# An attention tower on one core: ones beside x in the weighing products, the projection one step later, and the second variance on ScalarE

## What is computed

```
h = tok(x)                      # 16 -> 512 (silu) -> 256, plus a linear residual 16 -> 256
h = h + attention(layernorm(h)) # 16 heads of 16 over the 64 tokens of a sequence, then W_out
h = h + ffn(layernorm(h))       # fft -> complex matrix -> ifft: one real 256 x 256 product, plus bias
```

## Time and profile before

| | |
|---|---|
| median of 3 runs | 142.65 us (142.65 to 142.79) |
| the profiled execution | 142.76 us |
| its span, first to last instruction | 141.0 us |
| mean granted TensorE clock | 0.993 |
| busy: PE, PEld | 132.8 us, 112.4 us |
| busy: DVE, ACT, POOL | 111.6, 85.7, 94.7 us |

### The profile page before, as it was taken

The page is one execution under the profiler, slowest core; times in us unless marked ns, Lnnn a source line. Parts: engine busy times, 40 slices in busy tenths (PEclk is TensorE's granted clock), DMA queues, the critical chain, the costliest instruction groups (busy, mean ns, idle before and its releaser), DMA issues.

```text
span 141.0 us, 6132 instructions
## 1 busy us (share of the span) xinstructions
PE 132.8 (94%) x2444; PEld 112.4 (80%) x2444; DVE 111.6 (79%) x337; ACT 85.7 (61%) x245; POOL 94.7 (67%) x186
## 2 busy tenths in 40 slices
PE   6879999999999998999999999999999999999861
PEld 2469999999997876978878889889788788788540
DVE  5584596859978578798898898988988988978751
ACT  4374765477878584865947747649558477455110
POOL 3284796996583364677687686786876876773361
PEclk9999999999999999999999999999999999999997
DMA  4678000030000010121312302203113123031102
GB/s 70 157 174 257 14 0 0 0 36 11 2 0 5 5 19 5 19 50 15 63 37 23 60 12 49 56 7 65 46 15 60 37 23 59 6 60 41 38 0 74
DMA packets 24508, 5.89 MB, mean 42 GB/s; under 512 B 20384, under 2 KB 24224, under 8 KB 24480
## 3 DMA queue, kind: packets, MB, share of 16 engines
q1 hardware_dynamic: 24192, 5.37, 18.3%
q10 hardware_dynamic: 288, 0.13, 0.3%
HBM read 2.35 MB, written 2.10 MB: 32 GB/s over the span
## 4 chain that ended last, share of the span: by engine, by line
PE 78%; DVE 7%; POOL 4%; issue 3%; DMA 3%; ACT 1%; SPq 1%; POOLq 0%; DVEq 0%
PE bank L1036 11%; PE bank L954 11%; PE bank L1022 7%; PE bank L1099 6%; PE bank L1075 5%; PE bank L959 5%; PE bank L1080 4%; PE bank L1120 4%; PE bank L1064 3%; DMA wf_raw<-in_W_r 3%; PE bank L1049 2%; PE bank L1133 2%; PE bank L948 2%; PE bank L1103 2%; PE bank L1124 2%
## 5 line engine op out<-in xcount | busy, mean ns | idle before, releaser
L824 DVE TENSOR_REDUCE bank<-bank 128x4 f32<-128x256 f32 x64 | 22.8, 425 | 6.9 <-ACT pT L376 6.5
L376 ACT ACTIVATE pT<-bank 128x256 f32<-128x256 f32 x64 | 19.4, 391 | 2.5 <-PE bank L1049 2.5
L1036 PE MATMUL bank<-qT,xzT 32*128 32x64 f32 x512 | 17.9, 276 | 0.0
L1036 PEld LDWEIGHTS bank<-qT,xzT 32*128 32x128 f32 x512 | 15.7, 186 | 2.7 <-issue 2.7
L695 DVE TENSOR_TENSOR hid_lo<-bank,hid_hi 128x512 fp32r<-128x512 f32 x16 | 11.0, 685 | 7.5 <-ACT bank L344 7.5
L582 POOL TENSOR_TENSOR side_lo<-sideT,side_hi 128x256 fp32r<-128x256 f32 x14 | 10.2, 728 | 8.3 <-ACT sideT L386 8.3
L545 POOL TENSOR_SCALAR xblk<-xh,parity_sb 128x128 f32<-128x128 f32 x32 | 11.5, 372 | 5.9 <-PE bank L1080 4.8
L371 ACT ACTIVATE maxT<-bank 128x128 fp32r<-128x128 f32 x16 | 4.4, 277 | 17.8 <-PE bank L1058 17.8
L593 POOL TENSOR_TENSOR on_lo<-onT,on_hi 128x256 fp32r<-128x256 f32 x14 | 10.3, 737 | 7.1 <-ACT on_hi L390 6.8
L553 POOL TENSOR_TENSOR hb_all<-h_all,bout_bc 128x256 f32<-128x256 f32 x16 | 11.5, 735 | 4.0 <-ACT h_all L348 4.0
L361 ACT ACTIVATE xzT<-bank,parity_sb 128x256 f32<-128x256 f32 x28 | 12.0, 498 | 0.0
(11 more groups left out here) (166 smaller groups left out, 386.8 us busy)
## 6 DMA issues: line engine op xcount, KB each, us to landing
out<-y SPq DMA_DIRECT2D x16, 128.0 KB, 1.7
xblk<-xh SPq DMA_DIRECT2D x32, 32.0 KB, 2.5
wo_raw<-in_W_o SPq DMA_DIRECT2D x1, 512.0 KB, 4.2
wout_raw<-in_W_out SPq DMA_DIRECT2D x1, 256.0 KB, 2.9
fr<-in_wr SPq DMA_DIRECT2D x1, 256.0 KB, 4.3
fi<-in_wi SPq DMA_DIRECT2D x1, 256.0 KB, 4.3
minus_raw<-in_minus_rows SPq DMA_DIRECT2D x1, 128.0 KB, 2.2
bout_bc<-in_b_out SPq DMA_DIRECT2D x1, 128.0 KB, 3.5
```

The costliest lines, as they stand in the source:

```text
L376: nc.scalar.activation(pT[:, j, :], bank[j][:, D:2 * D], ACT.Exp).then_inc(exp_done, 1)
L824: nc.vector.tensor_reduce(rowmax[:, j, :], bank[j][:, 0:D].rearrange("p (h k) -> p h k", k=TOK), AX_X, ALU.max).then_inc(max_done, 1)
L1036: pe.matmul(bank[j][:, at0:at0 + TOK], xzT[t % 3][rows32, 2 * half + b, :, :].rearrange("p e k -> p (e k)"), qT[t % 3][rows32, half, TOK * ...
```

## The change

The change does the following.

- In `weigh` the separate row sums go. `xblk` keeps ones in the 16 columns beside each head's 16 columns of x, so each product gives the weighted x and the row sum together. The products are now 64 rows deep, one for each head e of a pair: 32 with 64 columns in place of 16 with 64 and 4 with 256. They write two banks. All of `xblk` is placed by four DMAs a tile; `place_same` on GpSimd goes.
- The division: VectorE transposes all 512 columns at once and takes reciprocals (`invert`), GpSimd multiplies (`divide`; VectorE from tile 14 on), VectorE transposes back (`turn_on`). The two small steps on VectorE, spread and multiply, go.
- `project(i)` moves from the middle of step i to the start of step i+1, directly behind `weigh(i+1)`. `mix_freq` and `finish` move back a step or more: mix_freq(i-2), finish(i-3). `turn_max` stands between `scores` and `keyed_scores`, and `turn_side` ahead of `weigh`. Tiles 14 and 15 are caught up in step 15 and behind it.
- The variance of h2 goes from VectorE (`variance2`) to ScalarE, in two passes with an accumulated sum: `sum_row`, then `sum_squares` with the negative mean as a per-partition bias; `mean2` on GpSimd stands between them.
- The order in a step changes on ScalarE and GpSimd too, and `xh`, `h2b`, `rstd2` get a third buffer.

```diff
...
-        X_BANK, PV_BANK, MAX_BANK, PROJ_BANK = 4, 5, 6, 7
-        FREQ_BANK, SIDE_BANK, QUERY_BANK = PROJ_BANK, MAX_BANK, X_BANK
-        rowmax = bank[MAX_BANK][:, P:P + 4 * QUADS].rearrange("p (j h) -> p j h", h=4)
+        PV_BANK = (5, 6)
+        QUERY_BANK, SIDE_BANK, MAX_BANK, PROJ_BANK, FREQ_BANK = 4, 4, PV_BANK[1], 7, 7
+        rowmax = score_banks[:, :, 0:4]
...
+        def turned_x(t):
+            return bank[4][:, 0:D] if t < 3 else bank[PV_BANK[0]][:, D:2 * D]
...
-            def place_crossed(t):
+            def place(t):
                 sp.wait_ge(xh_set, t + 1)
                 if t >= 2:
                     sp.wait_ge(pv_done, t - 1)
+                heads = xh[t % 3][:].rearrange("p (g e d) -> p g e d", e=2, d=HD)
                 for b in range(2):
...
+                    for e in range(2):
+                        sp.dma_start(xblk[t % 2][TOK * e:TOK * e + TOK, b, :, 0:HD],
+                                     heads[TOK * b:TOK * b + TOK, :, e, :]).then_inc(xblk_placed[t % 2], 16)
+            sp.wait_ge(blocks_set, 2)
+            place(0)
+            place(1)
+            for i in range(T + 3):
                 if i + 2 < T:
-                    place_crossed(i + 2)
-                if i >= 1:
-                    store(i - 1)
+                    place(i + 2)
+                if i >= 3:
+                    store(i - 3)
...
+            def sum_row(t):
+                act.wait_ge(h2_done, t + 1)
+                if t >= 1:
+                    act.wait_ge(mean2_done, t)
+                    act.wait_ge(squares2_done, t)
+                nc.scalar.activation(unread[:], h2[t % 2][:], ACT.Copy, accum_out=sum2[:]).then_inc(sum2_done, 1)
+            def sum_squares(t):
+                act.wait_ge(mean2_done, t + 1)
+                act.wait_ge(sum2_done, t + 1)
+                if t >= 1:
+                    act.wait_ge(ve2_done, t)
+                nc.scalar.activation(unread[:], h2[t % 2][:], ACT.Square, bias=neg_mean2[:],
+                                     accum_out=squares2[:]).then_inc(squares2_done, 1)
             def step(i):
+                if i + 3 < T:
+                    copy_xT(i + 3)
                 if i + 1 < T:
                     copy_max(i + 1)
+                if i + 3 < T:
+                    copy_xzT(i + 3)
+                if i >= 1:
+                    sum_row(i - 1)
+                if i + 1 < T:
+                    exponent(i + 1)
+                if i < WHOLE_ON:
+                    lead_on(i)
+                if i + 3 < T:
+                    copy_q(i + 3)
                 if i >= 1:
                     copy_side(i - 1)
-                if i + 3 < T:
-                    copy_xT(i + 3)
-                    copy_xzT(i + 3)
-                if i < WHOLE_ON:
-                    lead_on(i)
-                if i + 1 < T:
-                    exponent(i + 1)
-                if i + 3 < T:
-                    copy_q(i + 3)
+                    sum_squares(i - 1)
...
-            def place_same(t):
...
+            def mean2(t):
+                pool.wait_ge(sum2_done, t + 1)
+                if t >= 1:
+                    pool.wait_ge(squares2_done, t)
+                nc.gpsimd.tensor_scalar(neg_mean2[:], sum2[:], -1.0 / D, None, ALU.mult).then_inc(mean2_done, 1)
             def inv_std2(t):
-                pool.wait_ge(mv2_done, t + 1)
-                nc.gpsimd.tensor_scalar(ve2[:], mv2[:, 1:2], EPS, None, ALU.add).then_inc(ve2_done, 1)
-                if t >= 2:
-                    pool.wait_ge(y_set, t - 1)
+                pool.wait_ge(squares2_done, t + 1)
+                if t >= 1:
+                    pool.wait_ge(rstd2_done, t)
+                nc.gpsimd.tensor_scalar(ve2[:], squares2[:], 1.0 / D, EPS, ALU.mult, ALU.add).then_inc(ve2_done, 1)
+                if t >= 3:
+                    pool.wait_ge(y_set, t - 2)
...
+            def divide(t):
+                pool.wait_ge(inv_done, t + 1)
+                nc.gpsimd.tensor_tensor(on_rows[:].rearrange("p c e d -> p e c d"), weighedT[:, :, :, 0:HD],
+                                        inv_sum[:].unsqueeze(3).to_broadcast([P, 2, D // 32, HD]),
+                                        ALU.mult).then_inc(on_divided, 1)
             def step(i):
-                if i + 2 < T:
-                    place_same(i + 2)
                 if i == 0:
                     split_mix_weights()
-                if 1 <= i <= WHOLE_SIDE:
-                    split_side(i - 1)
+                if i < WHOLE_ON:
+                    divide(i)
+                if 2 <= i <= WHOLE_SIDE + 1:
+                    split_side(i - 2)
+                if 2 <= i <= T:
+                    inv_std2(i - 2)
+                if 1 <= i < T:
+                    add_bias(i - 1)
+                    mean2(i - 1)
+                if i + 4 < T:
+                    normalize(i + 4)
                 if i < WHOLE_ON:
                     split_on(i)
                 if i == T:
+                    mean2(i - 1)
                     add_bias(i - 1)
                     inv_std2(i - 1)
-                elif i >= 1:
-                    inv_std2(i - 1)
-                    add_bias(i - 1)
-                if i + 4 < T:
-                    normalize(i + 4)
...
+            def invert(t):
+                dve.wait_ge(pv_done, t + 1)
+                if t >= 1:
+                    dve.wait_ge(on_divided, t)
+                nc.vector.transpose(weighedT[:].rearrange("p e c r -> p e (c r)"), weighed[:, :, 0:D]).then_inc(pv_turned, 1)
+                dve.wait_ge(pv_turned, t + 1)
+                nc.vector.reciprocal(inv_sum[:], weighedT[:, :, :, HD]).then_inc(inv_done, 1)
             def divide(t):
-                dve.wait_ge(pv_done, t + 1)
-                nc.vector.transpose(sumsT[:], bank[PV_BANK][:, D:2 * D]).then_inc(sums_turned, 1)
...
                 dve.wait_ge(inv_done, t + 1)
...
+                if t == WHOLE_ON:
+                    dve.wait_ge(on_set, t)
+                nc.vector.tensor_tensor(on_rows[:].rearrange("p c e d -> p e c d"), weighedT[:, :, :, 0:HD],
+                                        inv_sum[:].unsqueeze(3).to_broadcast([P, 2, D // 32, HD]),
+                                        ALU.mult).then_inc(on_divided, 1)
+            def turn_on(t):
+                dve.wait_ge(on_divided, t + 1)
                 if t >= 1 and t - 1 < WHOLE_ON:
                     dve.wait_ge(on_lo_set, t)
                 elif t >= 1:
                     dve.wait_ge(proj_done, t)
-                nc.vector.tensor_tensor(onT[:].rearrange("p a t -> p (a t)"), bank[PV_BANK][:, 0:D],
-                                        inv_rows[:], ALU.mult).then_inc(on_set, 1)
+                nc.vector.transpose(onT[:].rearrange("p a t -> p (a t)"),
+                                    on_rows[:].rearrange("p c e d -> p (c e d)")).then_inc(on_set, 1)
...
-            def variance2(t):
...
             def step(i):
-                if i < T:
+                invert(i)
+                if i >= WHOLE_ON:
                     divide(i)
                 if i >= 1:
-                    variance2(i - 1)
+                    residual(i - 1)
+                if i >= 3:
+                    finish(i - 3)
+                turn_on(i)
                 if i + 3 < T:
                     split_x(i + 3)
                 if i + 2 < T:
                     for j in range(QUADS):
                         maximum(i + 2, j)
                     split_max(i + 2)
-                if i < T:
-                    residual(i)
-                if i >= 1:
-                    finish(i - 1)
-
...
+            finish(T - 3)
+            residual(T - 1)
+            finish(T - 2)
+            finish(T - 1)
...
             def weigh(t):
                 pe.wait_ge(exp_done, QUADS * (t + 1))
-                pe.wait_ge(xblk_same, t + 1)
-                pe.wait_ge(xblk_crossed[t % 2], 32 * (t // 2 + 1))
+                pe.wait_ge(xblk_placed[t % 2], 64 * (t // 2 + 1))
                 if t == 0:
                     pe.wait_ge(h_copied, T)
-                for j in range(QUADS):
-                    pe.matmul(bank[PV_BANK][32 * j:32 * j + 32, D:2 * D], pair_ones[:], pT[:, j, :], start=True, stop=True)
                 for half in range(HALF):
                     for b in range(2):
                         cols = slice(half * P + TOK * b, half * P + TOK * (b + 1))
-                        for j in range(QUADS):
-                            last = pe.matmul(bank[PV_BANK][32 * j:32 * j + 32, cols],
-                                             xblk[t % 2][:, b, half * P + 32 * j:half * P + 32 * j + 32],
-                                             pT[:, j, cols], start=True, stop=True)
+                        for e in range(2):
+                            for j in range(QUADS):
+                                last = pe.matmul(bank[PV_BANK[e]][32 * j:32 * j + 32, cols],
```

(62 more changed lines are left out.)

128 lines of the change are left out of this document (49 added, 79 removed).

## The result

The changed kernel takes 146.94 us (median of 4 runs, 146.17 to 148.26), the kernel before 142.65 on the same chip: ratio 1.0303, 95% interval 1.0239 to 1.0366. It is slower. The forecast was slower too, at 144.5, but the time lies just outside its range of 140.8 to 146.9. The profiled execution took 146.17 with a span of 144.4; outside the span lie 1.77 us, as before. Executions over 1.5% above the fastest of the same kernel are left out of ratios and medians.

What follows compares the result with a forecast made beforehand. TensorE bounds the kernel, in flight 94% of the span, 5.56 us a step. Span 141.0 + 0.1 (steps) - 1.2 (filling) + 3.0 (emptying) = 142.9, with 1.76 around it 144.66, so about 144.5; range 140.8 to 146.9.

Steps and rivals of the forecast that it cites:

- Filling: Start of the pipeline, to the weighing of tile 13: 1.2 us earlier than before, bounds 0 and 2.
- Emptying: From the end of weighing 13 to the last y: 19.45 us against 16.45, +3.0, bounds +1.5 and +3.8.
- Placing: Four placing DMAs a tile in SyncE's queue, 2.5 us: covered by up to 5.27 - 2.5 us of room, costing nothing.
- The loop that I expect to set the step: Two-step loop through ScalarE, VectorE and GpSimd to project: 11.13 us, 5.57 a step, so TensorE waits at on_lo.
- TensorE in the change: TensorE's own pieces in a step: 5.56 - 0.44 + 0.15 = 5.27 us, up to 5.74.
- 64 x 7 ns = 0.43: Weighing's 64 new instructions on eight array pieces, at half of 14 ns each: 0.43 us, other bound 0.90.
- 0.15 for the change of pieces: TensorE, each change from one kind of array piece to another: pieces behind it about 0.15 us longer.
- Its 0.40: ScalarE's sum_row ahead of the exponentials: taken as 0.40 us, between 0.33 and above 0.60.
- TensorE sets the pace: First rival, 22%: the loop sums to less than 10.54, the step is 5.27, time 140.9 us; sign, unbroken TensorE pieces.
- Weighing at 14 ns: Rival, 15%: issue limits weighing to 14 ns an instruction, TensorE's step is 5.74, time 146.6 us.

Runs made afterwards that it cites:

- x6_tail: Changed kernel with step 14 alone reordered, among other moves project(14) ahead of weigh(15): 145.14 us, ratio 1.017 to the kernel before.
- x1_bn: Changed kernel with the second variance back on VectorE, without sum_row, sum_squares and mean2: 145.95 us, ratio 1.0257 to the kernel before.
- x5_place2: Changed kernel without two of the four placing DMAs for tiles from 2 on, work incomplete: 146.5 us, ratio 1.0269 to the kernel before.
- x3_halfweigh: Changed kernel without the weighing products of each pair's second head (e = 1), work incomplete: 143.70 us, ratio 1.0086 to the kernel before.
- x7_bnhalf: Changed kernel without the e = 1 weighing products and with the second variance back on VectorE, work incomplete: 142.76 us, ratio 1.0001 to the kernel before.
- x13_pool: Changed kernel with three more small operations on GpSimd ahead of split_on, results unused: 148.25 us, ratio 1.0376 to the kernel before.
- x10_double: Changed kernel with each weighing product issued twice, 128 instructions a tile, same result: 170.36 to 174.43 us in four executions.

## Why the prediction was right in its sign and wrong in its size

Its sum for the profiled execution was 144.66; it took 146.17.

- **Filling**: forecast -1.2, measured -0.91 by weighing 2. Held, 0.3 off.
- **Emptying**: forecast +3.0, measured +3.16, along the path as written. Held. x6_tail shows that 1.1 of it is order and can be had back; x1_bn, that the variance on ScalarE is only 0.13 of it.
- **Placing**: hidden, as forecast (x5_place2).
- **The step that failed** is "The loop that I expect to set the step". The loop is there, and its terms were good: x3_halfweigh, where it binds, has 10.94 against 11.13, and most of the difference is `divide`, whose start to the next is 0.58 in place of 0.72. But it does not set the step. TensorE's own pieces do, and the forecast had these too short.
- **TensorE in the change**, 5.27 in the forecast, is 5.56 with the exponentials out of the way (x1_bn). The mis-sized term is "64 x 7 ns = 0.43": the 64 instructions take 0.64. The burst of eight that the forecast took its rate from is real and is seen again, but only for the first 32 instructions of a tile (0.24 us); the second 32 take 0.40. The other term of weighing, 0.15 for the change of pieces, held. Of the rest of the 0.29, 0.06 is the change ahead of `project`, which costs 0.21 against its old place behind `mix_freq`, not 0.15. So the reordering costs 0.21 and weighing saves 1.02 - 0.79 = 0.23. The 0.44 of the forecast less its 0.15 became nothing.
- **ScalarE** with `sum_row` in the way adds 0.06. The forecast saw the two engines level at the exponentials and put `sum_row` into the loop, but not at TensorE's own next piece, the weighing. Its 0.40 was right: the start of sum_row to that of the exponentials is 103.05 - 102.65.

```profile
102.65 0.43 ACT L411 ACTIVATE unread<-h 128x256 f32<-128x256 f32 x1
102.96 0.22 ACT L411 ACTIVATION_READ_ACCUMULATOR unread<-h 128x1 f32 x1
103.05 1.23 ACT L383 ACTIVATE pT<-score_banks 128x256 f32<-128x256 f32 x4
```

So a step of 5.57 was forecast from 11.13 / 2, and 5.62 came from 5.56 + 0.06. The two numbers agree because the errors happen to meet, not because the reason was right: the unbroken pieces are what the forecast had named as the sign of its first rival. That rival, *TensorE sets the pace*, was right in its mechanism, and its 5.27 wrong. *Weighing at 14 ns* gave 146.6, the nearest time, but not by what happened: it had all 64 instructions at 14 ns and the weighing piece at 1.05, and they take 10 ns on average and 0.79. It was right in that the pace of the burst did not last.

Of the 1.5 us between sum and profile 0.5 are the step (+0.6 over the middle in place of +0.1), 0.53 the pause in step 10, 0.3 the filling and 0.15 the end. The pause, a late packet of instructions, was nowhere in the forecast. Another 0.8 lie between the profiled execution and the median of its four runs; on the other chip the median was 146.25. Here the changed kernel spreads more than the one before does (145.59 to 148.26 over both chips, against 142.28 to 142.79 on the same two). The longest execution had a mean granted clock of 0.98, but the next, of 147.27, had 1.0, so the clock is not all of it, and why is open.

The Trainium skill (TensorE: Matmul & The Clock Gate, Part 1) puts starts of small matmuls no closer than about 25 ns. The trace does not agree: at the head of a weighing they come 7 ns apart, and 64 of them within 0.64 us (x1_bn). The Trainium skill (TensorEngine Tiling (Array Packing), Key Properties) says that a change of mode drains the engine, and gives no price. The trace agrees that the pieces behind such a change are longer, by 0.15 at the transposes and at weighing and by 0.21 at `project`.

## What to carry to other kernels

A rate read in a short burst is the rate of a burst. Here eight instructions showed 7 ns each, and 64 in a row cost 10: price a long group by a group that is as long, or keep the bound for it in the forecast. And when a change makes one kind of piece cheaper on the engine that sets the pace, price the borders as well: the one new border, 0.21, ate the 0.23 that weighing saved. When an experiment leaves work out, ask what else it changes: x3_halfweigh and x7_bnhalf halved both the instructions and the part of the array in use, so the difference of the pieces, 6.6 ns an instruction, is no instruction's price. Two candidates for the pace that differ by a few per cent (10.54 and 11.13 here) are not ordered by a forecast; an experiment that shortens one and one that lengthens the other (x3_halfweigh, x13_pool) does it in two runs. Moving work one step later cost 3.2 us at the end of a pipeline of 16 steps and gave back 0.9 at its start: over the 11 steps between, it pays only from 0.2 us a step on.

## What the hardware showed unexpectedly

- TensorE's instructions arrive in packets of 16 KB, 128 pairs of load and product. At 132 pairs in 5.56 us (24 per us) TensorE never paused for them. At 156 in 5.62, 28 per us, one packet was late enough in four of the nine traces to stop it for 0.5 to 0.8 us. With 220 in a step it stood still for 0.3 to 1.5 us, mostly at every second or third packet, and got through some 30 pairs per us. Each of these stops ends 1.1 to 1.6 us after a packet has landed; where the packet of step 10 landed 2.4 us or more before the product that needs it, there was none. Leaving out half of the placing DMAs does not move the stops of x10_double.
- Eight-piece weighing starts its first 32 instructions 7 ns apart and its second 32 about 12 ns apart (x1_bn); the next 64 cost 10 ns each (x10_double). On four pieces it is 14 ns throughout (x7_bnhalf and the kernel before).
- At the end of the pipeline, where TensorE is in flight for about half of the time, the granted clock fell to half for 3.4 us in the profiled execution of x7_bnhalf and not in that of x1_bn, and the end was some 1.4 us longer (20.84 against 19.48).
- An accumulated sum on ScalarE is two instructions, 0.43 and 0.22 for 256 columns, of which 0.40 stands in its queue.
